# Turning rows by DMA, masking with the maxima and moving the low parts in a fused sequence-model, attention and FFN kernel

## What is computed

```
h = concat(ssm(x), txt)                 # 32 batches of 205 rows (128 image + 77 text) of 1024
h = h + attn(layernorm(h))              # 32 heads, 8 KV heads, head size 32, causal, softmax
h = h + ffn(layernorm(h))               # one 1024 x 1024 matrix with a bias: W_base + a low-rank update
```

## Time and profile before

| | us |
|---|---|
| median of 3 runs (3077.54 to 3079.27) | 3078.82 |
| the profiled execution | 3082.04 |
| its span, first to last instruction | 3080.3 |
| TensorE busy | 2781.2 (90%) |
| VectorE busy | 1997.8 (65%) |
| ScalarE busy | 1094.1 (36%) |
| GpSimd busy | 1029.9 (33%) |

### The profile page before, as it was taken

One profiled execution on the slowest core, in us unless ns is written; L12 is line 12 of the kernel. 1 busy time (PEld: TensorE's weight loads), 2 busy tenths in 40 slices (PEclk: granted clock), 3 DMA queues, 4 the chain that ended last, 5 costly groups with the idle time before them and its releaser, 6 DMA issues. The chain is left out here.

```text
span 3080.3 us, 70678 instructions
## 1 busy us (share of the span) xinstructions
PE 2781.2 (90%) x27970; PEld 2030.8 (66%) x28224; DVE 1997.8 (65%) x4642; ACT 1094.1 (36%) x2362; POOL 1029.9 (33%) x1402
## 2 busy tenths in 40 slices
PE   0847799999999999999999986699999999999999
PEld 0736698989899898989898883244444444444444
DVE  8874577787787878777787865444444444444443
ACT  3331355555555555555555565211001101100110
POOL 4631254544545454554445454011101110110110
PEclk9977899999999999999999996599999999999999
DMA  5642422222222322222222223154554455455453
GB/s 179 194 116 69 103 58 78 58 75 78 57 76 60 80 58 77 69 65 77 56 76 58 69 49 144 55 122 120 129 137 123 121 133 132 118 127 137 124 122 86
DMA packets 446040, 297.32 MB, mean 97 GB/s; under 512 B 389416, under 2 KB 407976, under 8 KB 445232
## 3 DMA queue, kind: packets, MB, share of 16 engines
q1 hardware_dynamic: 445472, 282.69, 35.7%
q10 hardware_dynamic: 240, 10.09, 1.1%
HBM read 116.36 MB, written 80.61 MB: 64 GB/s over the span
## 5 line engine op out<-in xcount | busy, mean ns | idle before, releaser
L693 POOL TENSOR_SCALAR_AFFINE_SELECT p<-p 128x256 f32<-128x256 f32 (+1 forms) x768 | 334.3, 437 | 762.0 <-ACT p L720 743.6
L805 DVE TENSOR_REDUCE mx<-psS 77x2 f32<-77x410 f32 (+1 forms) x768 | 449.3, 613 | 181.9 <-PE psS L912 110.7
L930 PE MATMUL psJ<-xth,qh 128*128 128x205 f16 x2048 | 522.0, 255 | 24.9 <-DVE qsl L813 24.7
L932 PE MATMUL psJ<-xth,ql 128*128 128x205 f16 x2048 | 518.4, 253 | 0.0
L931 PE MATMUL psJ<-xtl,qh 128*128 128x205 f16 x2048 | 516.5, 252 | 0.0
L720 ACT ACTIVATE p<-psT,escale 128x410 f32<-128x410 f32 (+1 forms) x768 | 410.4, 570 | 276.2 <-PE psT L870 256.8
L698 POOL TENSOR_TENSOR pl<-p,ph 128x410 f16<-128x410 f32 (+1 forms) x512 | 447.7, 894 | 102.5 <-ACT ph L727 95.7
L1257 POOL TENSOR_TENSOR hb<-h,bias_sb 128x1024 f32<-128x1024 f32 x52 | 122.5, 2355 | 962.4 <-DVE h L1293 962.4
L1271 ACT CAST xh<-xn 128x1024 f16<-128x1024 f32 x52 | 54.4, 1045 | 967.1 <-DVE xn L1302 967.1
L1332 PE MATMUL ps5O<-woh,ath 128*128 128x512 f16 x832 | 316.2, 380 | 26.3 <-DMA atl<-al 26.3
L1293 DVE SCALAR_TENSOR_TENSOR h<-ps5O,osc,h_in 128x512 f32<-128x512 f32 x104 | 78.1, 751 | 402.4 <-PE ps5O L1334 402.4
(11 more groups left out here) (227 smaller groups left out, 5906.9 us busy)
## 6 DMA issues: line engine op xcount, KB each, us to landing
a_in<-acat SPq DMA_DIRECT2D x52, 512.0 KB, 3.8
h_in<-hcat SPq DMA_DIRECT2D x52, 512.0 KB, 4.7
qst<-qsh SPq DMA_DIRECT2D x512, 51.2 KB, 2.1
out<-y SPq DMA_DIRECT2D x51, 512.0 KB, 3.1
hcat<-ob SPq DMA_DIRECT2D x64, 256.0 KB, 4.0
xin<-hcat SPq DMA_DIRECT2D x32, 512.0 KB
acat<-ao SPq DMA_DIRECT2D x32, 512.0 KB
qst<-qsl SPq DMA_DIRECT2D x256, 51.2 KB, 2.1
```

Of the source, the lines that this page charges most:

```text
L693: pool.affine_select(out=v, in_=v, compare_op=ALU.is_ge, fill=0.0, base=0, pattern=[[0, v.shape[1]], [1, w]], channel_multiplier=-1).then_ ...
L805: dve.tensor_reduce(dst, v, AX.X, ALU.max).then_inc(s_read, 1)
L930: pe.matmul(ps[:, 0:S], wh[:, k, c], xth[:, par, k, :], start=k == 0, stop=False)
L932: m = pe.matmul(ps[:, 0:S], wl[:, k, c], xth[:, par, k, :], start=False, stop=k == KC - 1)
```

## The change

In the attention:
- The units `x` and TensorE's transposes go. In slots 3 and 4, after the units, ScalarE centres the rows (128 x 1024 and 77 x 1024) in place and writes their scaled float16 high part (`high_part`); VectorE writes the low part in slots 5 and 6 (`low_part`) and no longer scales the rows in slot 3. In slot 7, between the exponentials and the casts, ScalarE issues four DMA transposes (`turn`: high and low part of the 128 image rows, then of 80 rows that hold the 77 text rows). TensorE waits for all four at the top of the next step.
- Loads and stores move from SP to ScalarE: loads and the store of the second half of the heads to slot 2, the store of the first half to slot 6.
- The mask matmul of the image rows goes. VectorE takes the maximum of each of the four heads with the mask added in the same instruction (four `tensor_tensor_reduce` of 128 columns for one `tensor_reduce` of 4 x 128).
- The low part of piece 0 moves from VectorE to GpSimd.
- `norm` has one reciprocal and one product for both kinds of rows.

In the sequence model: sizes are made by 32 + 4 small exponentials on ScalarE with a per-partition scale; the phases are rounded with two rounds on VectorE, and |.| and sine on ScalarE give the four tables; VectorE multiplies all four by their sizes; `SUMMED` goes, so that every channel has two matmuls.

The core of the diff:

```
@@ ssm, tables
-            pool.wait_ge(ab_ok, 1)
-            for k in range(2):
-                pool.tensor_tensor(size[:, k], per_row(a[:]), per_step(iqr[:, k, :]), ALU.mult).then_inc(size_arg, 1)
-            for t in range(2):
-                pool.wait_ge(sine_ok, t + 1)
-                pool.tensor_tensor(tab[:, t], tab[:, t], size[:, 0], ALU.mult).then_inc(tab_ab, 1)
+            act.wait_ge(ab_ok, 1)
+            for k in range(2):
+                for r in range(LR):
+                    m = act.activation(size[:, k, :, r], a[:], ACT.Exp, scale=iqr[:, k, r:r + 1])
+                m.then_inc(size_ok, 1)
...
+            chain(dve.tensor_scalar(tab[:, 0], base, phase[:, 0:1], ROUND, ALU.add, ALU.add))
+            dve.scalar_tensor_tensor(turned[:, 0], tab[:, 0], ROUND, base, ALU.subtract,
+                                     ALU.subtract).then_inc(frac_ok, 1)
...
+            dve.wait_ge(size_ok, 2)
+            dve.wait_ge(sine_ok, 4)
+            for t in range(4):
+                dve.tensor_tensor(tab[:, t], tab[:, t], size[:, t // 2], ALU.mult).then_inc(tab_ok, 1)
@@ ssm, chunks
-                chain(m)
-                dve.tensor_tensor(es[:, ch % 2, 0, 0:SUMMED], es[:, ch % 2, 0, 0:SUMMED],
-                                  es[:, ch % 2, 1, 0:SUMMED], ALU.add).then_inc(e_ok, 1)
-                    last = 0 if j < SUMMED else 1
-                    for k in range(last + 1):
+                    for k in range(2):
@@ attention, gpsimd
+            pool.memset(xfh[:, 1, :], 0.0)
+            pool.memset(xfl[:, 1, :], 0.0)
...
-                    for k in (1, 2):
+                    for k in range(3):
                         pool.wait_ge(hi_done, 24 * b + 3 * g + k + 1)
                         pool.tensor_tensor(view(pl, g % 2, k), view(p32, g % 2, k), view(ph, g % 2, k),
                                            ALU.subtract).then_inc(lo_pool, 1)
@@ attention, scalar
+            def high_part(b, par, t):
+                r, x = T[t], xin[0:T[t], 1 - par, t, :]
+                if t == 0:
+                    act.wait_ge(ln_done, b + 4)
+                    if b >= -2:
+                        act.wait_ge(xt_in[par], 64 * ((b + 2) // 2 + 1))
+                act.activation(x, x, ACT.Identity, bias=nmean[0:r, t:t + 1]).then_inc(centred, 1)
+                act.wait_ge(centred, 2 * (b + 3) + t + 1)
+                act.activation(xfh[0:r, t, :], x, ACT.Copy, scale=rs[0:r, 3, t:t + 1]).then_inc(x_hi, 1)
+
+            def turn(t, to, n):
+                r, cols = ((P, slice(0, P)), (TROWS, slice(P, P + TROWS)))[t]
+                act.wait_ge(x_hi, 2 * n + t + 1)
+                act.dma_start_transpose(out=xth[:, to, :, cols], in_=xfh[0:r, t, :]).then_inc(xt_in[to], 16)
+                act.wait_ge(x_lo, 2 * n + t + 1)
+                act.dma_start_transpose(out=xtl[:, to, :, cols], in_=xfl[0:r, t, :]).then_inc(xt_in[to], 16)
...
                 for g in SLOTS:
+                    if g == 2 and has["load"]:
+                        wait(act, x_lo, 2 * (b + 3))
+                        load(b + 4, par)
+                    if g == 2 and has["last"]:
+                        store(b - 1, 1)
+                    if g == 6 and has["att"]:
+                        store(b, 0)
                     (three exponentials)
+                    if g == NKV - 1 and has["ln"]:
+                        wait(act, pj_filled, base)
+                        for t in range(2):
+                            turn(t, 1 - par, b + 3)
                     (three casts, the units' high parts)
+                    if g in (3, 4) and has["ln"]:
+                        high_part(b, par, g - 3)
@@ attention, vector
+            def low_part(b, par, t):
+                r = T[t]
+                dve.wait_ge(x_hi, 2 * (b + 3) + t + 1)
+                dve.scalar_tensor_tensor(xfl[0:r, t, :], xin[0:r, 1 - par, t, :], rs[0:r, 3, t:t + 1], xfh[0:r, t, :],
+                                         ALU.mult, ALU.subtract).then_inc(x_lo, 1)
...
                     if k == 0:
-                        v, dst = src[:].rearrange("p (h i) -> p h i", i=P), mx[:, 0, 4 * j:4 * j + 4]
+                        for r in range(REP):
+                            m = dve.tensor_tensor_reduce(seen[:, r, :], src[:, r * P:(r + 1) * P], mask[:, 0, :], 1.0, LEAST,
+                                                         ALU.add, ALU.max, mx[:, 0, 4 * j + r:4 * j + r + 1])
+                        m.then_inc(s_read, 1)
...
-                        dve.wait_ge(hi_done, 24 * b + 3 * g + 1)
-                        dve.tensor_tensor(view(pl, g % 2, 0), view(p32, g % 2, 0), view(ph, g % 2, 0),
-                                          ALU.subtract).then_inc(lo_done, 1)
+                    if has["ln"] and g in (5, 6):
+                        low_part(b, par, g - 5)
@@ attention, tensor
-                    pe.matmul(ps[:], ident_bf[:], mask[:], start=True, stop=False, skip_group_check=True)
...
-                    for k in range(4):
-                        c = 4 * half + k
-                        m = pe.transpose(ps[:, k * r:(k + 1) * r], xin[0:r, 1 - par, t, c * P:(c + 1) * P], ident[0:r, 0:r])
+                if has["qkv"]:
+                    pe.wait_ge(xt_in[par], 64 * ((b + 2) // 2 + 1))
```

More of the change, by code:

```diff
@@ L205, in _ @@
             act.activation(dt[:], ldt[:], ACT.Exp).then_inc(dt_ok, 1)
+            act.wait_ge(ab_ok, 1)
[3 more added lines that the diff above has]
+                m.then_inc(size_ok, 1)
+            for la in range(LA):
+                m = act.activation(ela[:, la, :], a[:], ACT.Exp, scale=ila[:, la:la + 1])
+            m.then_inc(la_exp_ok, 1)
             act.wait_ge(args_ok, 1)
@@ L252, in _ @@
             chain = Chain(dve, dve_c)
-            for t, (top, bottom) in enumerate(((0.25, 0.25), (0.5, 0.0), (0.25, 0.0), (0.0, 0.25))):
-                dve.memset(phase[0:N, t:t + 1], top)
-                m = dve.memset(phase[N:P, t:t + 1], bottom)
+            for half, back in ((slice(0, N), 0.0), (slice(N, P), -0.25)):
+                dve.memset(phase[half], back)
+                dve.memset(lag[half], back * TWO_PI)
+            m = dve.memset(quarter[:], 0.25 * TWO_PI)
             chain(m)
@@ L274, in _ @@
             chain(dve.tensor_scalar(f[:], b[:], tp, None, ALU.mult))
-            for k in range(2):
-                dve.tensor_tensor(bases[k], per_row(f[:]), per_step(iqr[:, k, :]), ALU.mult).then_inc(base_ok, 1)
             for k, src in enumerate((a, b)):
@@ L376, in _ @@
                         pe.wait_ge(k_read, n - 3)
-                    last = 0 if j < SUMMED else 1
-                    for k in range(last + 1):
+                    for k in range(2):
                         m = pe.matmul(ps[n % 4][:, j % 2, :], u[:, ch % 2, j].rearrange("p a c -> p (a c)"),
-                                      es[:, ch % 2, k, j, :], start=k == 0, stop=k == last)
+                                      es[:, ch % 2, k, j, :], start=k == 0, stop=k == 1)
                     if j % 2:
@@ L456, in attention @@
     T = (P, TXT)
+    TROWS = 80
     with ExitStack() as ctx:
@@ L463, in attention @@
         xin = sb("xin", [P, 2, 2, D])
-        xth, xtl = sb("xth", [P, 2, KC, S], F16), sb("xtl", [P, 2, KC, S], F16)
+        xfh, xfl = sb("xfh", [P, 2, D], F16), sb("xfl", [P, 2, D], F16)
+        xth, xtl = sb("xth", [P, 2, KC, P + TROWS], F16), sb("xtl", [P, 2, KC, P + TROWS], F16)
         qsh, qsl = sb("qsh", [P, KC, S], F16), sb("qsl", [P, KC, S], F16)
@@ L513, in units @@
                     row.append(("m", 1))
-                if s >= 4 and has["ln"]:
-                    row.append(("x", s - 4))
                 if s == 4 and has["max"]:
@@ L613, in step @@
                     shift_rows(1, par)
-                if has["load"]:
-                    wait(sp, pj_filled, base)
-                    load(b + 4, par)
                 if b == -1:
@@ L621, in step @@
                         sp.dma_start(dst, src).then_inc(arrived, 16)
-                if has["last"]:
-                    store(b - 1, nxt)
                 if has["qkv"]:
@@ L746, in norm @@
                 n = 8 * b + g
-                if g == 0:
-                    wait(dve, a_out[par], 16 * (b - par))
+                if g % 4 == 0:
+                    wait(dve, a_out[g // 4], 32 * b)
                 dve.wait_ge(av_done, n + 1)
```

159 lines of the change are left out of this document (71 added, 88 removed).

## The result

The changed kernel takes 3296.6 us (median of 4 runs, 3285.7 to 3309.9) against 3079.1 before: a ratio of 1.071 (95% interval 1.066 to 1.075), **217 us slower**. The forecast was 3220 with a range up to 3290: the right sign and the right mechanism, too small by a third. The profiled execution took 3285.7 (span 3283.9), 203.6 more than the one of before.

What follows compares the result with a forecast made beforehand. TensorE was taken to bound the attention, with SP's queue a close limit. Steps +132, tail +13.5, attention start +8 and sequence model −12 made +141 on 3082.0, so 3223, median 3220; 8-in-10 range 3095 to 3290, own range 3180 to 3270.

Steps and rivals of the forecast that it cites:

- The step: Attention step with a norm: 3.4 − 0.75 + 1.9 = +4.55 us, in 29 steps +132.
- The turn: Slot 7: four DMA transposes in a row on ScalarE leave TensorE 4.4 us idle at the next step's top.
- ScalarE in slots 4 to 6: Row passes of 2.05 us delay exponentials; TensorE loses 1.15 and 1.05 us in slots 4 and 5, none in slot 6.
- Slots 0 to 3: First half of a step: −0.9 for four masks, −0.3 K wait, +0.45 for loads and stores: −0.75 us.
- The clock: Behind the stall at a step's start: half speed in three steps of four, 1.9 us a step.
- The sequence model: Before the attention: tables −17, loop of 16 chunks +5 for its added matmuls, together −12 us.
- The start of the attention: First projection later, behind ScalarE's high parts, VectorE's low parts and the first transposes: +8 us.
- The tail: Steps 30 and 31: a third low part on GpSimd lengthens each of 16 slots by 0.85: +13.5 us.
- Rival B: Top of each step: transposes issue like plain loads, the step gains 0.75 to 1.2 us; 3053 us; chance 0.17.
- Rival A: Top of each step: the transposes stall TensorE but the clock stays; 3165 us; chance 0.20.
- Rival C: Transposes beside the stacking DMAs cost 2 us each, land after 5: +4.4 us a step, 3350 us; chance 0.10.

Runs made afterwards that it cites:

- experiment 1: The changed kernel with the four DMA transposes done only in the first two steps, later rows computed from old data; 3078.4 us, ratio 1.001.
- experiment 2: The changed kernel with the DMA transposes, ScalarE's row passes and VectorE's low parts of the rows only in the first two steps; 3032.6 us, ratio 0.986.
- experiment 3: The changed kernel with 24 unused 512-column matmuls ahead of TensorE's wait at the top of each step; 3247.9 us, ratio 1.056.
- experiment 7: The kernel before with only the changed kernel's sequence model; 3062.3 us, ratio 0.996.
- experiment 11: The kernel before with the new sequence model (all its matmuls), the image rows' mask on VectorE and the merged norm; 3036.1 us, ratio 0.9864.
- Experiment 9: The kernel before with only the first low part of each head group moved from VectorE to GpSimd; 3094.1 us, ratio 1.004.
- Experiment 6: The changed kernel with the text rows' two transposes issued ahead of the image rows' two; 3306.6 us, ratio 1.076.

## Why the prediction came out too small

The step's sum is what failed, and in it the sizes of four terms, not the mechanism. The turn was priced with the text rows' first issue at 1.0 us; the row passes' waits were taken to end with slot 5; the masks taken off slots 0 to 3 were counted as shorter slots, one for one; and the half clock was taken for three steps in four.

**The step, +4.55 forecast, +7.50 measured** by the shift (+7.66 by the starts of the steps). This is the mean length of each slot over steps 1 to 27, from one slot's first scores to the next slot's:

| us | slot 0 | 1 | 2 | 3 | 4 | 5 | 6 | 7 | step |
|---|---|---|---|---|---|---|---|---|---|
| before | 7.68 | 7.12 | 6.62 | 7.61 | 5.96 | 4.96 | 4.79 | 4.79 | 49.52 |
| after | 9.41 | 6.97 | 7.08 | 7.69 | 5.86 | 5.67 | 4.62 | 9.89 | 57.18 |
| experiment 1 (no turn) | 7.33 | 6.97 | 7.44 | 7.69 | 5.86 | 5.67 | 4.65 | 4.27 | 49.89 |
| experiment 2 (no passes either) | 8.87 | 6.97 | 7.48 | 7.69 | 4.42 | 4.45 | 4.24 | 4.24 | 48.36 |
| experiment 3 (full clock) | 7.14 | 6.97 | 7.08 | 7.69 | 5.86 | 5.67 | 4.56 | 10.27 | 55.25 |

Against 49.6 + 4.55 the step is 3.0 us too long, and the four terms give it:
- *The turn*, slot 7 with its stall: 8.7 by the forecast (4.27 + 4.4), 9.89 measured, **+1.2**. The start and the landing were right to 0.2 us (2.31 us into the slot in the step shown, and the last part is there 3.0 us after its issue on average). The fourth issue begins 4.54 us behind the first, not 3.65. Wrong was the text rows' issue, "80 rows, taken as 1.0": it costs no less than the larger one, 1.31 us, and where it meets a code load up to 2.3. The step shown, with 10.41, is such a case. The trace of before had a warning: the other pair of transposes of the output stage, of the same 128 x 1024 float16, had held SP's queue for longer than the pair in the earlier trace rows (ns, min/median/max):

```profile
L1217 SPq DMA_TRANSPOSE atl<-al x52: 1383/2304/4329, 1992.2 to 3027.8; - x52
```

- *ScalarE in slots 4 to 6*: 5.86, 5.67, 4.62 for 5.6, 5.35, 4.25, **+0.95**. A pass takes 1.15 us, not 1.045, and the waits that the passes cause in the step shown are 1.25 and 1.04 us (forecast 1.15 and 1.05). The mechanism is as forecast, but slot 6 is held up too: it is 4.24 only in experiment 2, without the passes.
- *Slots 0 to 3*: −0.75 forecast, −0.1 measured at full clock (28.88 in experiment 3 for 29.02), **+0.5**. Slots 0 and 1 are shorter by 0.54 and 0.15, much as forecast. Slot 2 is 0.46 longer with the loads' and stores' issues in it, for 0.23 (0.45 less a mask). Slot 3 is 0.08 longer instead of 0.22 shorter: in experiment 1 it is 7.69 with 6.55 busy, and TensorE waits 1.1 us behind VectorE for a projection bank (`psJ <- DVE qsl`), so what leaves TensorE there turns idle.
- *The clock*: 1.9 forecast. Slot 0, which carries it, is 9.41 for the 7.14 of experiment 3, 2.3 us, **+0.4**; the clock falls in every step and not in three of four. The Trainium skill ("TensorE: Matmul & The Clock Gate", Part 1) has the array throttled after idleness and released by activity; experiment 3 agrees.

**The sequence model, −12:** −14.8 (experiment 7). The tables are ready 16.8 us sooner (−17 forecast): the first matmul starts at 62.9 for 79.7. The chunks then cost 1.8 us more than before, not 5, since 512 matmuls without a gap take 7.05 us a chunk and not 7.2:

```profile
62.90 112.81 PE L380 MATMUL ps<-es,u 128*128 128x256 f32 x512 [62.90 <-DVE u L364]
```

**The start of the attention, +8:** the first projection is at 243.79, and at 236.14 in experiment 11, which keeps TensorE's transposes. So +7.7:

```profile
243.79 0.33 PE L955 MATMUL psJ<-xth,qh 128*128 128x205 f16 x1 [68.08 <-DMA xtl<-xfl]
```

```profile
236.14 0.35 PE L934 MATMUL psJ<-xth,qh 128*128 128x205 f16 x1 [0.23 <-DVE xtl L818]
```

**The tail, +13.5:** about +6, half of the forecast. Step 30 takes 35.5 us for 33.5 and step 31, the last, 33.1 for 29.05. Experiment 9, which has only the third low part on GpSimd, has 35.4 and 33.7, so this part of the change does it, surely in step 31 (28.6 to 29.1 us in every run with two low parts a group); step 30 is 33.5 to 36.0 among those runs, so its 2 us may be none of it. GpSimd is the bound in the last step: it is busy without a break after the change, and had a tenth of the time free before.

```profile
1866.00:1892.00 26.00, 18.05 (x312) 10.42 (x311) 10.10 (x41) 22.14 (x48) 23.37 (x41) 0.51 0.10 35
2084.00:2115.00 31.00, 18.48 (x314) 10.74 (x314) 5.38 (x18) 22.72 (x49) 30.93 (x50) 0.50 0.09 29
```

**Not foreseen: 19 us back after the attention.** The code there is the same. The start of the output stage has a stretch at half clock in every kernel, and its length differs: 75.0 us before, 30.7 us after (all stretches behind the last shift together 126 and 113). TensorE works 48.7 us in the one and 4.4 in the other, and what it does there takes twice as long:

```profile
1924.80:1999.80 75.00, 48.67 (x99) 19.01 (x98) 38.23 (x44) 19.49 (x26) 0.35 (x1) 0.50 0.18 50
```

```profile
2173.10:2203.80 30.70, 4.36 (x11) 1.61 (x12) 16.50 (x20) 10.51 (x10) 0.35 (x1) 0.50 0.47 116
```

Experiment 6, the same work, has 143 us of such stretches and its part behind the last shift is 1290.7 for 1271.0. So this is not an effect of the change. Of the fourteen traces three have the short stretch (the changed kernel, experiments 1 and 2), and there the part behind the last weigh takes 1166 to 1168 us; in the others, with 75 to 79 us, it takes 1185 to 1189. The times of one kernel show the same step: the eight of experiment 1 are 3067 to 3070 and 3087 to 3089, and its trace, of a run of 3070, is one of the short ones. What sets the length stays open. Two things follow. With outputs of the same length the change costs about 223 us in the traces and not 204. And a median of a few runs is sure to some 20 us only, not to the 6 us that the prediction named, so the smaller gains and losses below 20 us rest on many runs and on the steps in the traces.

**What held.** The place and the kind of the loss: TensorE idle for the transposed rows at the top of each step (5.48 us on average, 4 to 5 forecast), and the half clock behind it. Rival B (transposes as cheap to issue as plain DMAs) is out: the issuing queue is held 1.3 to 2.8 us by a transpose and 0.34 to 0.62 by a load or store. The sentence of the Trainium skill ("Advanced Engine Details and Errata", X-Bar Transpose (TRN2)) that transpose DMAs are as fast as regular ones does not hold for this queue; for the landing nothing here speaks against it, since these transposes of up to 256 KB land after 3.3 us (median) and the page of the changed kernel has 4.0 us for the stores `hcat<-ob` of 256 KB. Rival A is out, since the clock fell. Rival C (2 us an issue, landing after 5) is out as a rule: the issues are 1.4 us on average, and the last part lands after 3.0. GpSimd's 33.1 us a step was forecast as 32. VectorE did not become the bound of the step. The forecast's own range, 3180 to 3270, was too narrow: it allowed one term of the step to be off, and four were, all to the same side.

## What to carry to other kernels

Where an engine both computes and issues DMAs, count each issue with its whole duration: the four transposes held ScalarE for 5.7 us a step, more than the 1.6 us that the prediction estimated for TensorE's own transposes, and moving them earlier hid the landing and most of the half clock, but not the issues. Work taken off a busy engine shortens a slot only where that engine's last instruction ends the slot; find what ends each slot before you count the saving, since here 2.3 us of freed TensorE time a step turned idle as long as ScalarE's passes stood in the way. And take such a change apart: three of its parts gain 1.4% together, and one loses 7%.

## What the runs showed of the hardware

- A DMA transpose of 80 rows holds ScalarE's queue as long as one of 128 rows (medians 1.30 to 1.45 us). In 11 of 28 steps one of the first three in a row takes 1.7 to 2.5 us, and each of these 11 meets a 16 KB packet of the queue `q8 instruction` (5 of the other 117 do).
- With stalls of 5.5 us on average the granted clock fell in 29 of 29 steps (half for 6.8 us a step), with stalls of 3.1 us in 23 of 29 (3.9 us); matmuls whose result nobody reads, in place of the stall, kept it full.
- The half-clock stretch at the start of the output stage is 30.7 us in three traces and 75 to 79 us in eleven, with the same code, and is worth some 20 us.
- An add and maximum in one VectorE instruction over 128x128 from PSUM takes 0.286 us. Four of them, 1.14 us, cost VectorE more than the plain 512-column maximum (0.688 us), and the kernel still gains, since the mask's matmul leaves TensorE.
